# Mixing across channels as four fp32 products of 128 columns instead of a three-term float32r split, in a two-layer convolution and expert network

## The reference, cut to what matters

```python
# layer 0: x = x + ffn0(conv(x) + context + bias)       (grouped convolution, 9 taps)
# layer 1:
h   = gelu(cond @ W0 + b0); h = gelu(h @ W1 + b1)
att = softmax(h @ W2 + b2)                                # [128, 8]
agg_w = einsum('bk,koi->boi', att, weight[..., 0])        # a 32 x 32 matrix for each sample
mixed = einsum('boi,bih->boh', agg_w, x) + (att @ bias_k)[:, :, None]
# ffn (both layers), for the tokens t of its input v:
#   logits = v @ W_router.T; the two largest of 8 give the weights w
#   out = v @ W_base.T + b_base + 2 * sum_e w[t, e] * (v @ A[e].T) @ B[e].T
x = x + ffn1(mixed)
```

## Time and profile before

| | |
|---|---|
| median of 3 runs | 393.58 us (393.46 to 393.81) |
| profiled execution | 393.21 us, span 391.4 us |
| TensorE matmul, weight load | busy 383.4 us (98%), 373.5 us (95%) |
| VectorE, ScalarE, GpSimd | busy 277.9 us (71%), 218.6 us (56%), 225.3 us (58%) |
| granted TensorE clock | 1.00 in all 40 slices |
| DMA | 79 GB/s over the span |

### The profile page before, as it was taken

The page is one execution under the profiler, slowest core; times in us unless marked ns, Lnnn a source line. Parts: engine busy times, 40 slices in busy tenths (PEclk is TensorE's granted clock), DMA queues, the critical chain, the costliest instruction groups (busy, mean ns, idle before and its releaser), DMA issues.

```text
span 391.4 us, 9197 instructions
## 1 busy us (share of the span) xinstructions
PE 383.4 (98%) x2793; PEld 373.5 (95%) x2793; DVE 277.9 (71%) x988; ACT 218.6 (56%) x593; POOL 225.3 (58%) x199
## 2 busy tenths in 40 slices
PE   7989999999999999999999999999999999999996
PEld 6779999999999999999999999999999999999985
DVE  3887767767766777676677777667677767767764
ACT  4856545565554555555565555456555545565451
POOL 3298466655556656555665655666555566655560
PEclk9999999999999999999999999999999999999999
DMA  7861222121222212222211222221212222121101
GB/s 269 312 140 42 82 82 79 33 82 54 81 81 81 59 49 74 61 81 81 81 56 52 60 75 81 81 81 42 66 56 79 81 81 79 29 81 54 56 28 55
DMA packets 19885, 31.04 MB, mean 79 GB/s; under 512 B 5984, under 2 KB 6272, under 8 KB 19872
## 3 DMA queue, kind: packets, MB, share of 16 engines
q1 hardware_dynamic: 19872, 30.89, 25.8%
HBM read 21.95 MB, written 8.91 MB: 79 GB/s over the span
## 4 chain that ended last, share of the span: by engine, by line
PE 90%; DVE 4%; issue 2%; ACT 1%; POOL 1%; DMA 1%; SPq 1%; DVEq 0%; ACTq 0%
PE ps_out L348 32%; PE ps_out L360 22%; PE ps_conv L315 11%; PE ps_out L380 11%; PE ps_mix L396 5%; PE ps_t L327 3%; PE ps_mix L399 2%; PE ps_out L407 1%; PE ps_t L367 1%; DVE yT L677 1%; PE ps_out L367 1%; DMA mix<-mix_nat 1%; DVE lb_w L689 1%; SPq L270 0%; DVE wa L677 0%
## 5 line engine op out<-in xcount | busy, mean ns | idle before, releaser
L348 PE MATMUL ps_out<-wa,yT 128*128 128x392 f32 x768 | 152.0, 345 | 0.9 <-ACT yT L507 0.7
L348 PEld LDWEIGHTS ps_out<-wa,yT 128*128 128x128 f32 x768 | 131.4, 188 | 4.4 <-ACT yT L507 0.9
L954 POOL TENSOR_TENSOR x_part<-x,x_part 128x512 fp32r<-128x512 f32 x31 | 40.1, 1293 | 114.4 <-ACT x_part L507 114.4
L360 PE MATMUL ps_out<-wb,yT 128*128 128x256 f32 x768 | 102.8, 283 | 0.0
L360 PEld LDWEIGHTS ps_out<-wb,yT 128*128 128x128 f32 x768 | 94.7, 189 | 0.0
L507 ACT ACTIVATE yT<-ps_t 64x256 fp32r<-64x256 f32 x128 | 48.4, 378 | 28.3 <-PE ps_t L327 25.9
L380 PE MATMUL ps_out<-lb_w,hwT 128*128 128x256 f32 x384 | 58.4, 288 | 0.5 <-ACT hwT L507 0.4
L677 DVE TENSOR_TENSOR yT<-ps_t,yT 64x256 fp32r<-64x256 f32 x128 | 53.7, 419 | 3.6 <-ACT yT L507 0.6
L315 PE MATMUL ps_conv<-x_part,conv_w 128*128 128x256 f32 x384 | 51.8, 284 | 0.0
L967 POOL TENSOR_TENSOR x1b<-x,base_bias 128x512 f32<-128x512 f32 x29 | 37.4, 1291 | 24.7 <-DVE res L810 24.7
L380 PEld LDWEIGHTS ps_out<-lb_w,hwT 128*128 128x128 f32 x384 | 49.7, 189 | 1.4 <-ACT hwT L507 0.6
(11 more groups left out here) (99 smaller groups left out, 504.0 us busy)
## 6 DMA issues: line engine op xcount, KB each, us to landing
x_raw<-in_x_phase SPq DMA_DIRECT2D x32, 260.0 KB, 2.7
x_tok<-in_x_tok SPq DMA_DIRECT2D x32, 256.0 KB, 2.6
out<-res SPq DMA_DIRECT2D x31, 256.0 KB, 2.1
wa_raw<-in_wa SPq DMA_DIRECT2D x2, 784.0 KB, 6.9
wb_raw<-in_wb SPq DMA_DIRECT2D x2, 512.0 KB, 7.7
lb_raw<-in_lb SPq DMA_DIRECT2D x2, 256.0 KB, 8.1
bias<-in_bias SPq DMA_DIRECT2D x2, 256.0 KB, 7.3
scratch<-mix_nat SPq DMA_DIRECT2D x1, 512.0 KB, 3.7
```

What stands on the lines that cost most here:

```text
L348: last = mm(out_banks(y, t)[:, 0, 0:AR + DH], yT[y][dp][:, k, :], wa[y][:, wp, k, :], start=(n == 0 and k == 0), stop=(n == len(SPLITS) - ...
L360: last = mm(out_banks(y, t)[:, 1, OUT], yT[y][dp][:, k, :], wb[y][:, wp, k, :], start=(n == 0 and k == 0), stop=False, skip_group_check=True)
L954: g.tensor_tensor(x1_part[LO][:, :], x1[:, :], x1_part[HI][:, :].bitcast(F32), ALU.subtract).then_inc(s["x1l"], 1)
```

## The change

The mixing product takes x1 and the mixing matrix as they are, in fp32: for each of the four pieces one matmul with the piece of x1 as the stationary operand and 128 columns of `mix`. The results fill one bank of PSUM, and nothing is to be added to them. The split copies, the subtractions, the copy and the sum of the cross term, and their tiles and semaphores go. The product waits for x1 itself, and for the first two tiles for the DMAs that bring `mix`, which ScalarE waited for. `middle` waits until the previous mixing product is done, since that now reads x1. The matmuls that keep TensorE busy read a zero tile of their own.

```diff
-        x1_part = [sb(f"x1_part{p}", [P, D], F32R) for p in range(2)]
-        mix_part = sb("mix_part", [P, 2, P], F32R)
-        cross = sb("cross", [P, KT, P])
+        zeros = sb("zeros", [P, D], F32R)
...
-        def mixed(part):
-            return ps_mix[:, :, :].rearrange("p b (k w t) -> p (b k) w t", w=2, t=P)[:, :, part, :]
+        def mixed():
+            return ps_mix[:, 0, :].rearrange("p (k t) -> p k t", t=P)
+
+        def mixing(t):
+            return mix[:, bass.ds(t * SPT, SPT), :].rearrange("p a b -> p (a b)")
...
             def mix_product(t):
                 need(pe, s["yl"][1], t)
-                pe.wait_ge(s["mh"], t + 1)
-                pe.wait_ge(s["ml"], t + 1)
-                pe.wait_ge(s["x1h"], t + 1)
-                pe.wait_ge(s["x1l"], t + 1)
+                pe.wait_ge(s["x1"], t + 1)
+                if isinstance(t, int) and t < 2:
+                    pe.wait_ge(mix_first if t == 0 else mix_loaded, 16 * SPT)
                 for k in range(KT):
-                    b, c = divmod(k * 2 * P, 512)
-                    mm(ps_mix[:, b, c:c + 2 * P], x1_part[HI][:, k * P:(k + 1) * P],
-                       mix_part[:, :, :].rearrange("p a b -> p (a b)"), start=True, stop=False,
-                       skip_group_check=True)
-                    last = mm(ps_mix[:, b, c:c + P], x1_part[LO][:, k * P:(k + 1) * P], mix_part[:, HI, :],
-                              start=False, stop=True, skip_group_check=True)
+                    last = mm(ps_mix[:, 0, k * P:(k + 1) * P], x1[:, k * P:(k + 1) * P], mixing(t), start=True, stop=True)
                 last.then_inc(s["mix"], 1)
...
             # ScalarE
             def turned1(t):
-                act.wait_ge(s["y1"], t + 1)
+                act.wait_ge(s["mix"], t + 1)
                 need(act, s["base"][1], t)
-                copy(yT[1][HI][:, :, :], mixed(0)).then_inc(s["yh"][1], 1)
+                copy(yT[1][HI][:, :, :], mixed()).then_inc(s["yh"][1], 1)
             def step(t, has):
                 weigh(0, t)
                 if has(-2):
                     turned_hw(1, t - 2)
-                save_cross(t - 1)
                 turned1(t - 1)
-                split_mix(t)
                 if has(2):
                     split_x(t + 2)
                 turned_hw(0, t)
                 turned0(t + 1, 0)
                 turned0(t + 1, 1)
-                split_x1(t)
                 weigh(1, t - 1)
                 pass_bias(t)
...
             # VectorE, middle(t)
-                need(dve, s["x1h"], t)
-                need(dve, s["x1l"], t)
+                need(dve, s["mix"], t)
...
             # GpSimd, step(t)
                 form_base_bias(t - 1)
                 form_xb(t)
                 form_x1b(t - 1)
-                split_mix(t)
-                split_x1(t)
                 if has(2):
                     split_x(t + 2)
```

More of the change, by code:

```diff
@@ L180, in build @@
         mix_first = sem("mix_first")
-        names = ["xh", "xl", "xb", "conv", "y0", "t0", "x1", "x1h", "x1l", "x1b", "mh", "ml",
-                 "mix", "cross", "y1", "passed", "bb", "out"]
+        names = ["xh", "xl", "xb", "conv", "y0", "t0", "x1", "x1b", "mix", "passed", "bb", "out"]
         s = {n: sem("s_" + n) for n in names}
@@ L406, in keep_busy @@
                 for _ in range(count):
-                    mm(ps_out[0][:, 0, :], x1_part[HI][:, 0:P], x1_part[HI][:, :], start=True, stop=True)
+                    mm(ps_out[0][:, 0, :], zeros[:, 0:P], zeros[:, :], start=True, stop=True)
             keep_busy(9)
@@ L546, in turned0 @@
                     copy(dst, src).then_inc(s["yh"][0], 1)
[L548 to L551, removed]
             def save_sums():
@@ L567, in pass_bias @@
                                      scale=mix_bias[:, bass.ds(t, 1)]).then_inc(s["passed"], 1)
[L569 to L572, removed]
             def turned_hw(y, t):
@@ L577, in turned_hw, with turned1 @@
                 copy(hwT[y][HI][:, :], ps_hwT[y]).then_inc(s["hwh"][y], 1)
-            def save_cross(t):
+            def turned1(t):
                 act.wait_ge(s["mix"], t + 1)
-                need(act, s["y1"], t)
-                copy(cross[:, :, :], mixed(1)).then_inc(s["cross"], 1)
-            def turned1(t):
-                act.wait_ge(s["y1"], t + 1)
                 need(act, s["base"][1], t)
-                copy(yT[1][HI][:, :, :], mixed(0)).then_inc(s["yh"][1], 1)
+                copy(yT[1][HI][:, :, :], mixed()).then_inc(s["yh"][1], 1)
             def step(t, has):
@@ L632, in _ @@
             turned0(1, 1)
-            act.wait_ge(mix_first, 16 * SPT)
-            split_mix(0)
-            split_x1(0)
             high_wb(1)
             weigh(0, 1)
-            save_cross(0)
             turned1(0)
@@ L642, in _ @@
             pass_bias(0)
-            act.wait_ge(mix_loaded, 16 * SPT)
-            split_mix(1)
             split_x(3)
@@ L648, in _ @@
             turned0(2, 1)
-            split_x1(1)
             weigh(1, 0)
@@ L656, in _ @@
             turned_hw(1, LAST - 2)
-            save_cross(LAST - 1)
-            split_mix(LAST)
             turned_hw(0, LAST)
             turned1(LAST - 1)
-            split_x1(LAST)
             pass_bias(LAST)
             weigh(1, LAST - 1)
-            save_cross(LAST)
             turned1(LAST)
@@ L691, in low_lb @@
                                        op1=ALU.subtract).then_inc(lb_lo[y], 1)
-            v.memset(x1_part[HI][:, :].bitcast(F32), 0.0).then_inc(zeros_ready, 1)
+            v.memset(zeros[:, :].bitcast(F32), 0.0).then_inc(zeros_ready, 1)
             dve.wait_ge(conv_w_hi, 1)
@@ L848, in turned0 @@
                     low(dst, src, quarter(HI, hi, sample)[0].bitcast(F32)).then_inc(s["yl"][0], 1)
-            def sum_mixed(t):
-                dve.wait_ge(s["cross"], t + 1)
-                v.tensor_tensor(mixed(0), mixed(0), cross[:, :, :], ALU.add).then_inc(s["y1"], 1)
             def turned1(t):
                 dve.wait_ge(s["yh"][1], t + 1)
-                low(yT[1][LO][:, :, :], mixed(0), yT[1][HI][:, :, :].bitcast(F32)).then_inc(s["yl"][1], 1)
+                low(yT[1][LO][:, :, :], mixed(), yT[1][HI][:, :, :].bitcast(F32)).then_inc(s["yl"][1], 1)
             def step(t, has):
@@ L862, in step @@
                     turned_hw(1, t - 2)
-                sum_mixed(t - 1)
                 if has(-2):
@@ L898, in _ @@
             gate(0, 1)
-            sum_mixed(0)
             turned1(0)
@@ L913, in _ @@
             turned_hw(1, LAST - 2)
-            sum_mixed(LAST - 1)
             turned_hw(0, LAST)
@@ L918, in _ @@
             middle(LAST)
-            dve.wait_ge(s["x1h"], LAST + 1)
-            low(x1_part[LO][:, :], x1[:, :], x1_part[HI][:, :].bitcast(F32)).then_inc(s["x1l"], 1)
             choose(1, LAST - 1)
-            sum_mixed(LAST)
             gate(1, LAST - 1)
@@ L940, in split_x @@
                                 ALU.subtract).then_inc(s["xl"], 1)
[L942 to L945, removed]
             def form_xb(t):
@@ L950, in form_xb @@
                 g.tensor_tensor(xb[:, :], x_tok[:, :], bias[0][:, :], ALU.add).then_inc(s["xb"], 1)
[L952 to L955, removed]
             def form_base_bias(t):
```

## The result

The changed kernel takes 391.50 us, the median of 11 runs (389.63 to 392.05), against 393.32 us (392.45 to 393.81, 11 runs) before. The medians are 1.82 us apart. The ratio is 0.9949, with a 95% interval of 0.9938 to 0.9959, by which the changed kernel is about 2.0 us faster. The forecast was 392.4 us. The profiled execution took 390.74 us, its span is 388.9 us.

The account below looks back on a forecast made before the run. TensorE, busy throughout the loop, was taken to bound the kernel. Start -1.55, end -0.40 and loop +0.75 sum to -1.20 us, giving 392.4 us after moving to the median of three runs; range 391.0 to 395.2 us.

Parts of the forecast that it names:

- likeliest case: Whole kernel: the forecast itself, 391.3 to 392.8 us, given a 58% chance.
- The loop: Mixing product in thirty tiles: eight fp32 records take 0.90 us instead of 0.87, 0.025 us more a tile, +0.75 us.
- The column sums: Start: without GpSimd's two splits, TensorE's stall before the column sums goes altogether, 1.6 us.
- What is late next: Start: ScalarE's turned gate product, which the B-product waits for, moves forward by about the same; 1.55 us taken.
- The stall around 40 us: Start: one of the later short stalls there might go as well, giving the high end of 2.0 us.
- 1.55: Start: the gain taken in us, with a low end of 0.5 and a high end of 2.0.
- The end: Last tile: the last mixing product starts 0.41 us sooner and the chain moves with TensorE, -0.40 us, between 0.26 and 0.55.
- stall on leaving fp32: Behind each mixing product: 0.09 us lost before the next float32r load, 2.7 us in all, 395.1 us; chance 11%.
- better overlap: Run of eight records: load and stream overlap better, 0.1075 us a record, 390.7 us; chance 7%.
- the convolution's pace: Mixing product in the loop: 0.121 us a record, 0.97 us for eight, 394.6 us; chance 6%.
- columns on top: Mixing product in the loop: 1.06 us in place of 0.87, 0.19 us more a tile, 397.3 us; chance 4%.
- Start not gained: Start: gate product or VectorE's weight splits hold TensorE instead of GpSimd; 0.5 us left of 1.55, 393.4 us; chance 14%.

Follow-up runs that it names:

- tile 0 alone: The kernel before with the new fp32 mixing product for tile 0 only, all other tiles keeping the split: 391.99 us, ratio 0.9963.
- the last tile alone: The kernel before with the new fp32 mixing product for the last tile only, all other tiles keeping the split: 392.66 us, ratio 0.9978.
- 256 columns cut in two: The kernel before with each 256-column mixing matmul cut into two of 128, same columns, loads from 8 to 12 a tile: 406.01 us, ratio 1.0318.
- second profile: A further profile of the unaltered changed kernel, in an execution that took 392.05 us.

## Why the prediction was right, and where it was off

The direction and the place were right: nothing in the loop, one gain at the start, one at the end. The measured 391.50 us lies in the range and in the likeliest case's own 391.3 to 392.8. It is 0.9 us below the forecast: the kernel before took 0.26 us less than when the forecast was made, and the gain was 1.82 us instead of 1.20. By the steps:

- **The loop (+0.75 us forecast).** This is the term that was mis-sized; it measured nothing: 1.00 us a tile for product and transpose before and after, 2,411 matmuls in the same 321.75 us, and 332.71 us between the ends instead of 332.81. Eight records took 0.89 us, not 0.90, and the transpose saved its full 0.02 us. The reading behind it, that a weight load sets the pace of the float32r pairs, held, but the forecast stopped halfway. Both kernels have eight loads a tile, and the load also sets the pace of an fp32 record of 128 columns. Counted in loads the answer was no change at all. Counted in passes, 512 column passes more would have cost an estimated 0.21 us a tile; the trace shows them taking up the time that the loads take in any case. By the Trainium skill, FP8 and Floating Point Precision, TensorE Precision Notes, true fp32 is four passes; at 128 columns that did not tell the price.
- **The column sums (-1.6).** Right: 4.54 us after the same start instead of 6.23, 1.69 us sooner, though 1.3 against the three other profiles with the old start; with tile 0 alone it is 4.54 as well.
- **What is late next.** The place was right, the copy of the turned gates before the B-product. The statement that it moves by about as much was wrong in many runs. The prediction counted "one copy of x" among the work ahead of it on ScalarE as moving along, and did not look at what that copy waits for: a load that SP queues behind the mixing matrices' trip through HBM. Of 1.69 us, 0.82 and 0.78 are left at the B-product in two profiles and 1.64 in the first.
- **The stall around 40 us (named only for the high end, 2.0).** It was gone in the first profile of the changed kernel and there in the next two. With it gone and the load nearly on time the start gained 2.3 us (17.55 us from the product of tile 1 in layer 0 to that in layer 1 at 41.34, instead of 19.88), with both against it 0.8 us. Two kernels with the old start (the last tile alone, and 256 columns cut in two) took 19.52 us for the stretch; against them it is 2.0 and 0.4. So 1.55 lies between two kinds of runs, and no profile shows it: that the sum came near is luck in this term.
- **The end (-0.40).** Measured 0.54 us in the profile of the kernel with the last tile alone (14.81 instead of 15.35 us from the start of the tile to the end of the span), and as much in the changed kernel. 0.43 of it is the earlier start that was forecast; the rest is that the next product follows 0.81 us after the mixing product's start, not 0.95. The next stall is the one that was named.

The rivals: no stall on leaving fp32 showed (the float32r product starts 0.11 us behind the transpose, as elsewhere, and in the last tile, without a transpose, 0.81 us after the start of the eight records). The eight records took 0.89 us, not the 0.86 of *better overlap*, the 0.97 of the convolution's pace or the 1.06 of *columns on top*. *Start not gained* came true in part, by an engine, SP, that it did not name.

## What to carry to other kernels

Price short matmuls by the number of weight loads, not by columns or passes: here, below some 0.11 us of streaming, the load of a 128-column operand is what is paid. So a three-term split with two loads for a piece and plain fp32 with two cost the same, and the other engines get the split's work back for nothing; with three loads for a piece the split took 12.7 us more. Where one engine is full throughout, look for a change's gain at the ends of the program, and follow each instruction ahead of the next wait to what it waits for itself, the DMA queue included. A range of runs that is wide beside the gain is a finding: here most of it was one DMA behind a wait in SP's order.

## What the runs showed of the hardware that was not expected

VectorE's subtraction for the B weights, with both inputs in SBUF, takes 0.68 us when it starts first (36.58, changed kernel) and the GpSimd addition beside it takes 1.79 us instead of 1.29. When GpSimd starts first (36.67, second profile), it takes its 1.29 us, and VectorE's 1.56. The later one ends 1.14 and 0.55 us after the earlier, a little under its time alone (1.29 and 0.68), as if it had waited for the other to end. A few tenths of a us decide who pays. The stall around 40 us was there with 1.56 and not with 0.68. The Trainium skill, GPSIMD Engine Reference, Specifications, says that GpSimd shares its SBUF interfaces with VectorE, with contention where a VectorE instruction has two SBUF inputs; these rows agree, and show that the later one pays.
